# Node passes: new rows' transposes in banks of their own, aggregated rows' product at the pass's head, final rows copied ahead of the new normalisation

## The reference

```python
agg = segment_sum(alpha[:, :, None] * v[src], dst)          # first edge stage (attention)
embedding = agg.reshape(N, D) @ W0
h1 = _layer_norm(X + embedding, ln1_g, ln1_b)
ff = relu(h1 @ fc1_w + fc1_b) @ fc2_w + fc2_b                 # 128 -> 512 -> 128
x  = _layernorm(x + _layer_norm(h1 + ff, ln2_g, ln2_b))       # two normalisations in a row
# second edge stage: relu([x[src], edge_attr, req] @ W1 + b1) @ W2, summed by dst, both directions
# x[src] @ W1[:128] is formed once per node (y_tab) and gathered per edge
```

## Time and profile before

| | |
|---|---|
| Median of 3 runs | 2351.49 us (2351.31 to 2352.31) |
| The profiled execution's own time | 2351.63 us |
| Its span | 2349.8 us |
| First stage and attention edges | 0 to about 1137 us |
| Node passes | about 1137 to 1346.7 us |
| Second edge stage | 1346.7 us to the end |
| Mean granted TensorE clock | 0.77 of full speed |

### The profile page before, as it was taken

One profiled execution on the slowest core, in us unless ns is written; L12 is line 12 of the kernel. 1 busy time (PEld: TensorE's weight loads), 2 busy tenths in 40 slices (PEclk: granted clock), 3 DMA queues, 4 the chain that ended last, 5 costly groups with the idle time before them and its releaser, 6 DMA issues.

```text
span 2349.8 us, 31926 instructions
## 1 busy us (share of the span) xinstructions
PE 1416.0 (60%) x7352; PEld 1107.0 (47%) x7353; DVE 1439.1 (61%) x2963; ACT 742.3 (32%) x1515; POOL 1594.7 (68%) x1668
## 2 busy tenths in 40 slices
PE   5334655555555555555678566666666666666665
PEld 3134655555455555555566444444444444444443
DVE  2236977877877877878467444454554554554544
ACT  2143444344344344344366411111111111111111
POOL 4077777777777777776433277777777777777774
PEclk8667878777778778778799876877767777777776
DMA  5478555555555555555000122222222222222221
GB/s 166 127 180 275 174 157 165 162 156 164 163 156 166 161 156 164 162 156 154 11 33 33 47 60 63 65 63 63 65 64 62 65 64 63 64 64 65 62 64 46
DMA packets 149173, 255.39 MB, mean 109 GB/s; under 512 B 74829, under 2 KB 100097, under 8 KB 149005
## 3 DMA queue, kind: packets, MB, share of 16 engines
q0 software_dynamic: 65072, 160.39, 24.3%
q1 hardware_dynamic: 82194, 92.81, 12.8%
q10 hardware_dynamic: 1870, 1.78, 0.2%
HBM read 233.19 MB, written 28.04 MB: 111 GB/s over the span
## 4 chain that ended last, share of the span: by engine, by line
POOL 60%; issue 22%; PE 6%; DMA 5%; DVE 4%; ACT 2%; another core or an unknown queue 1%; POOLq 1%; DVEq 0%; ACTq 0%; PEldq 0%; SPq 0%
POOL arena L719 31%; POOL arena L662 29%; DMA kvq_tab<-arena 2%; PE ps L1120 2%; PE ps L1139 1%; DMA arena<-kvq_tab,arena 1%; PE ps L1079 1%; DMA arena<-in_src_dram 1%; ACT arena L875 1%; DVE arena L1508 1%; PE ps L1153 0%; DVE arena L1463 0%; PE ps L1115 0%; DVE arena L1525 0%
## 5 line engine op out<-in xcount | busy, mean ns | idle before, releaser
L662 POOL DMA_INDIRECT arena<-kvq_tab,arena x784 | 748.1, 954 | 266.4 <-issue 265.2
L719 POOL DMA_INDIRECT arena<-y_tab,arena x784 | 739.9, 944 | 251.9 <-issue 238.6
L1079 PE MATMUL ps<-arena 128*128 128x136 f32 x1568 | 314.0, 386 | 414.4 <-DVE arena L1463 414.4
L1079 PEld LDWEIGHTS ps<-arena 128*128 128x128 f32 x1568 | 304.3, 290 | 429.5 <-issue 429.5
L948 ACT ACTIVATE arena<-arena 128x512 f32<-128x512 f32 x224 | 123.3, 572 | 795.9 <-DVE arena L1596 795.9
L1596 DVE TENSOR_TENSOR arena<-ps,arena 128x512 f32<-128x512 f32 x224 | 134.7, 621 | 355.5 <-DMA arena<-y_tab,arena 352.5
L1225 PEld LDWEIGHTS ps<-arena 128*128 128x128 f32 x1568 | 268.3, 247 | 162.2 <-ACT arena L948 93.5
L1225 PE MATMUL ps<-arena 128*128 128x128 f32 x1568 | 289.7, 339 | 27.6 <-ACT arena L948 27.2
L1212 PE MATMUL ps<-w1blk,eaT 113*128 x456 | 255.8, 648 | 0.6 <-ACT eaT L943 0.6
L1409 DVE TENSOR_TENSOR arena<-ps,arena 128x512 f32<-128x512 f32 x224 | 137.8, 615 | 171.4 <-DMA arena<-kvq_tab,arena 163.8
L1055 PE MATMUL ps<-arena 128*128 128x128 f32 x1596 | 210.5, 285 | 44.5 <-ACT arena L811 27.7
(11 more groups left out here) (246 smaller groups left out, 1951.6 us busy)
## 6 DMA issues: line engine op xcount, KB each, us to landing
arena<-d SPq DMA_DIRECT2D x58, 897.0 KB
arena<-kvq_tab,arena POOLq DMA_INDIRECT x784, 2.8
arena<-y_tab,arena POOLq DMA_INDIRECT x784, 2.5
arena<-ea SPq DMA_DIRECT2D x60, 112.0 KB, 2.0
ea<-in_edge_attr_dram SPq DMA_DIRECT2D x2, 3125.0 KB, 19.1
y_tab<-arena SPq DMA_DIRECT2D x10, 625.0 KB
kvq_tab<-arena SPq DMA_DIRECT2D x6, 937.5 KB
arena<-kvq_tab SPq DMA_DIRECT2D x59, 64.0 KB
```

The lines of the kernel that those rows point to most:

```text
L662: g.indirect_dma_start(kv_s[:, r, t, :], None, kvq_tab.rearrange("n (a d) -> (n a) d", a=3), bass.IndirectOffsetOnAxis(ap=v3(idx, RING)[:, ...
L719: g.indirect_dma_start(yg_s[:, r, t, :], None, y_tab, bass.IndirectOffsetOnAxis(ap=v3(idx1, RING)[:, r, t:t + 1], axis=0)).then_inc(m_g[r] ...
L1079: last = mm(sums, hot_s[:, u, t, :], contrib_s[:, u, t * RW:(t + 1) * RW], start=(t == 0), stop=(t == G - 1))
```

## The change

- The transposes of `h1` go to banks 6 and 7, where the hidden blocks 1 and 3 also go, and wait for the relus of the pass before (`n_f1s`) where they waited for `n_xT`. ACT copies `nTh` from there.
- PE's product of the aggregated rows moves from between the hidden blocks to the head of the pass. It now waits for `n_xT` (banks 0 and 1 empty). For that ACT copies the rows of the next group (`nTa`) a pass earlier: after `res2` is normalised, ahead of the square root of the new group.
- ACT's copy of the transposed final rows (`nTx`) stands ahead of the normalisation into `h1`, where it stood behind it.
- `turn_rows` waits for the new semaphore `n_res` (DVE's add at line 1554 is done) and no longer for `n_v[0]` (its statistics are done), and for the copies of `y`.
- DVE's add at line 1554 waits for the copies of `y` as well.
- The loop runs six passes, and the seventh is written out, since its ACT part has no next group to copy. `s_bank` and `s_wu` are merged into `s_wq`.

```diff
-            with eng.Fori(0, GROUPS - 3) as i:
+            with eng.Fori(0, GROUPS - 4) as i:
                 one_pass(i + 3, i + 2, i + 1, i)
+            one_pass(GROUPS - 1, GROUPS - 2, GROUPS - 3, GROUPS - 4)
...
             def act_pass(new, mid, old, out_):
-                if new is not None:
+                if type(new) is int and new == 0:
                     a.activation(v3(nTa, GRP), by_tile(new), ACT.Copy).then_inc(n_aT, 1)
                 if mid is not None:
                     act.wait_ge(n_hTp, mid + 1)
-                    a.activation(nTh, bank(0, 2)[:, 0:GRP * P], ACT.Copy).then_inc(n_hT, 1)
+                    a.activation(nTh, bank(6, 2)[:, 0:GRP * P], ACT.Copy).then_inc(n_hT, 1)
...
+                if new is not None and not (type(new) is int and new == GROUPS - 1):
+                    act.wait_ge(n_emb, new + 1)
+                    a.activation(v3(nTa, GRP), by_tile(new + 1), ACT.Copy).then_inc(n_aT, 1)
                 if new is not None:
                     sqrt(0, new, norm1)
+                if old is not None:
+                    act.wait_ge(n_xTp, old + 2)
+                    act.wait_ge(n_x1c, old + 1)
+                    a.activation(nTx, bank(0, 2)[:, 0:GRP * P], ACT.Copy).then_inc(n_xT, 1)
+                if new is not None:
                     act.wait_ge(n_r[0], new + 1)
...
                     normalised(v3(h1, GRP), v3(res, GRP), norm1).then_inc(n_n1, 1)
-                if old is not None:
-                    act.wait_ge(n_xTp, old + 2)
-                    act.wait_ge(n_x1c, old + 1)
-                    a.activation(nTx, bank(0, 2)[:, 0:GRP * P], ACT.Copy).then_inc(n_xT, 1)
...
             def pe_pass(new, mid, old, out_):
+                if new is not None:
+                    if out_ is not None:
+                        pe.wait_ge(n_xT, out_ + 1)
+                        pe.wait_ge(n_ys, out_ + 1)
+                    if type(new) is int and 0 < new < 3:
+                        pe.wait_ge(n_res, new)
+                    pe.wait_ge(n_aT, new + 1)
+                    for t in range(GRP):
+                        last = mm(bank(0, 2)[0:NT, t * D:(t + 1) * D], nTa[:, t * NT:(t + 1) * NT], w0_sb[:, :])
+                    last.then_inc(n_emb, 1)
                 if mid is not None:
                     pe.wait_ge(n_n1, mid + 1)
-                    if out_ is not None:
-                        pe.wait_ge(n_xT, out_ + 1)
-                    transposes(h1, n_hTp)
+                    if not (type(mid) is int and mid == 0):
+                        pe.wait_ge(n_f1s, mid * FC)
+                    transposes(bank(6, 2), h1, n_hTp)
...
-                if out_ is not None:
-                    pe.wait_ge(n_ys, out_ + 2)
-                if new is not None:
-                    pe.wait_ge(n_aT, new + 1)
-                    for t in range(GRP):
-                        last = mm(bank(0, 2)[0:NT, t * D:(t + 1) * D], nTa[:, t * NT:(t + 1) * NT], w0_sb[:, :])
-                    last.then_inc(n_emb, 1)
...
-            def turn_rows(new, old):
-                if new is not None:
-                    pe.wait_ge(n_v[0], new + 1)
+            def turn_rows(new, old, out_):
+                if out_ is not None:
+                    pe.wait_ge(n_ys, out_ + 2)
+                if new is not None:
+                    pe.wait_ge(n_res, new + 1)
                 pe.wait_ge(n_x1, old + 1)
-                transposes(res2, n_xTp)
+                transposes(bank(0, 2), res2, n_xTp)
...
                     if mid is not None:
                         dve.wait_ge(n_n1, mid + 1)
-                    link(tt(r3, xg(new), v3(bank(0, 2)[:, 0:GRP * D], GRP), ALU.add))
+                    if out_ is not None:
+                        dve.wait_ge(n_ys, out_ + 2)
+                    tt(r3, xg(new), v3(bank(0, 2)[:, 0:GRP * D], GRP), ALU.add).then_inc(n_res, 1)
+                    dve.wait_ge(n_res, new + 1)
                     statistics(r3, n_v[0], norm1)
```

More of the change, by code:

```diff
@@ L251, in gnn_kernel @@
         s_tabi = [sem(f"s_tabi{l}") for l in range(2)]
-        s_dv = sem("s_dv"); s_wq = sem("s_wq"); s_init = sem("s_init"); s_bank = sem("s_bank"); s_wu = sem("s_wu")
+        s_dv = sem("s_dv"); s_wq = sem("s_wq"); s_init = sem("s_init");
         s_njc = sem("s_njc")
@@ L269, in gnn_kernel @@
         n_r = [sem(f"n_r{k}") for k in range(2)]
-        n_n1 = sem("n_n1"); n_xb = sem("n_xb")
+        n_n1 = sem("n_n1"); n_xb = sem("n_xb"); n_res = sem("n_res")
         n_b1 = sem("n_b1"); n_b1s = sem("n_b1s"); n_fc1 = sem("n_fc1"); n_hTp = sem("n_hTp")
@@ L986, in _ @@
             pe.wait_ge(s_const, 5)
-            pe.wait_ge(s_bank, 1)
-            pe.wait_ge(s_wq, 1)
+            pe.wait_ge(s_wq, 2)
             def pe_first(i):
@@ L1109, in _, with transposes @@
             pe.wait_ge(s_w4, 16 * (14 + 2 * (EG - 1)))
-            def transposes(src, done):
+            def transposes(to, src, done):
                 for t in range(GRP):
-                    last = tp(bank(0, 2)[:, t * P:(t + 1) * P], src[:, t * D:(t + 1) * D], ident[:, :])
+                    last = tp(to[:, t * P:(t + 1) * P], src[:, t * D:(t + 1) * D], ident[:, :])
                 last.then_inc(done, 1)
@@ L1136, in pe_pass @@
                     for t in range(GRP):
-                        if t == GRP - 1 and mid is not None:
-                            pe.wait_ge(n_hT, mid + 1)
                         last = mm(rows_y(t), nTx[:, t * P:(t + 1) * P], w1x[:, :])
@@ L1147, in pe_pass @@
                     hidden(mid, 1)
-                if out_ is not None:
-                    pe.wait_ge(n_ys, out_ + 2)
-                if new is not None:
-                    pe.wait_ge(n_aT, new + 1)
-                    for t in range(GRP):
-                        last = mm(bank(0, 2)[0:NT, t * D:(t + 1) * D], nTa[:, t * NT:(t + 1) * NT], w0_sb[:, :])
-                    last.then_inc(n_emb, 1)
-                if mid is not None:
                     for c in range(2, FC):
@@ L1158, in pe_pass @@
                         hidden(mid, c)
+                    if out_ is not None:
+                        pe.wait_ge(n_ys, out_ + 2)
                     for t in range(GRP):
                         if t == GRP - 2 and old is not None:
-                            turn_rows(new, old)
+                            turn_rows(new, old, out_)
                         for c in range(FC):
@@ L1269, in _ @@
             link = linker(dve, s_dv)
-            v.memset(ps[:, :], 0.0).then_inc(s_bank, 1)
+            v.memset(ps[:, :], 0.0).then_inc(s_wq, 1)
             dve.wait_ge(s_w, 48)
@@ L1362, in _ @@
             link(ts(epsc[:, :], epsc[:, :], 1.0, None, ALU.add))
-            ts(w2u[:, 2 * D:3 * D], w2wu[:, 2 * D:3 * D], epsc[:, :], None, ALU.mult).then_inc(s_wu, 1)
-            dve.wait_ge(s_wu, 1)
+            ts(w2u[:, 2 * D:3 * D], w2wu[:, 2 * D:3 * D], epsc[:, :], None, ALU.mult).then_inc(s_wq, 1)
+            dve.wait_ge(s_wq, 3)
             dve.wait_ge(s_init, 3)
```

## The result

The changed kernel takes 2342.61 us (median of 8 runs, 2340.02 to 2347.43); the kernel before took 2351.1 in its 8 runs beside it (2347.4 to 2352.31). The ratio worked out from the runs is 0.9974, with a 95% interval of 0.9964 to 0.9985: 6.1 us faster, between 3.5 and 8.5. (The two medians alone differ by 8.5 us, the far end of that interval.) On the 2351.49 of the forecast's basis that is 2345.4 us (2343.0 to 2348.0). The forecast was 2345.3.

A forecast was written before the change was run, and what follows sets the result against it. Bound: the chain from one group's `h1` to the next, with no engine full. Gains of 4.2 (six passes at 0.70), 1.7 (clock fall) and 0.4 (opening), 6.3 in all, take 2351.63 to 2345.3 us; range 2343.0 to 2349.0.

The forecast's parts named there:

- The steady pass: Loop passes of the node stage: period from 16.95 to 16.25, six times 0.70, 4.2 us in all.
- the extra copies: ACT's `nTa` (1.36) and `nTx` (0.68) ahead of `h1`: 0.6 of delay costs nothing, covered by POOL's L685.
- The 0.77 for the transposes: PE's transposes of `h1` in the steady pass before the change, given as 0.77 from start to start.
- The four hidden blocks: PE's hidden blocks in the changed steady pass, after `y`: 4.34, ending at 9.4 to 9.7.
- the wait added ahead of DVE's add: One more wait for DVE's add L1554 in each steady pass: worth up to 0.1, taken at 0.02.
- The fall of the clock: Half clock in the loop's second pass, 1.7 longer than its neighbours: taken to go, gaining 1.7.
- The earlier DVE: Rival: in steady passes L1518 starts before POOL's L690, period 0.26 shorter, six times 1.6, 2343.7; chance 0.10.
- The opening: Passes up to the third: transposes of `res2` start 0.3 earlier under `n_res`; gain 0.3 to 0.4, taken as 0.4.
- a rival, at 0.5: In the earlier-DVE rival (chance 0.10): half clock also ends sooner, so the opening may give 0.9, not 0.4: 2343.2.
- the seventh pass: Last of the six passes from the `h1` at 1199.44 to the last one, counted like the others at 0.70.
- The slower case: Rival: clock falls in every pass, period 18.95, six passes 10.3 longer, 2361.5; chance 0.05.
- the rival of a fall in another pass: The clock's fall stays or moves to another pass, price 1.7: 2346.2 to 2347.0; chance 0.20.

The follow-up runs named there:

- e3: Kernel before without POOL's addition of a bias to `h1c` (that part of the result missing); steady period 16.95, ratio to before 0.9989.
- e4: Changed kernel without POOL's addition of a bias to `h1c` (that part of the result missing); steady period 15.75, ratio to before 0.9947.
- e5: Kernel before with POOL's bias add to `xs` starting only after DVE's five-element instruction (one wait changed); period 15.94, ratio to before 0.9965.
- e6: Changed kernel with POOL's bias add to `xs` starting only after DVE's five-element instruction (one wait changed); period 15.78, ratio to before 0.9958.
- e10: The changed kernel run once more, nothing altered; steady period 16.27, ratio to before 0.9968.
- e1: Kernel before with only the transposes of `h1` in banks 6 and 7, product and ACT copies left in place; period 16.57, ratio to before 0.9989.
- e2: Changed kernel with ACT's copy of the final rows (`nTx`) behind the normalisation into `h1` again; period 17.46, ratio to before 1.0017.
- e7: Changed kernel with POOL's bias add a pass later and its copy into `nodes` after it, under DVE's statistics; period 15.25, ratio to before 0.9948.
- e8: e7 with the clearing of the second stage's two accumulators moved from POOL's first pass to its last; period 15.24, ratio to before 0.9913.
- e9: e8 with the copy of the next group's aggregated rows (`nTa`) on DVE instead of ACT; period 14.96, ratio to before 0.9924.
- e11: Changed kernel with PE's product of the aggregated rows put back between the hidden blocks; period 16.51, ratio to before 0.9998.

## Why the prediction was right, and where it was off

**The steady pass** came out as worked out, step by step. Transposes of `h1` at 2.16 (2.1 to 2.4 forecast), last relu at 9.77 (9.4 to 9.7, so it came 0.07 late), the data of the square root at 10.95 (10.98), the square root at 10.98 (11.03), the five instructions ending at 7.47 behind POOL's copy (7.49), the second square root 3.95 behind the first (3.95), L1525's counterpart ending with POOL's bias add (1231.17 and 1231.14), 5.28 from square root to `h1` (5.22), period 16.26 (16.25). That these agree for the reason given is shown by e3 and e4 (POOL's path binds after the change, not before) and by e5 and e6 (the bias add blocks 1.0 of 5.2, and it covers the 0.5 to 0.6 of the extra copies).

Three small terms in it were off and hardly show. The 0.77 for the transposes is a printed length and not, as the prediction says, from start to start, which is 0.61. The four hidden blocks take 4.65 from start to start and not 4.34, with the weights of a block waiting 0.25 for ACT's relu; both errors lie on the relu's side, which has slack. And the wait added ahead of DVE's add was taken at 0.02. Counted from the square root, the add starts at 0.92 where it started at 0.85, POOL's bias add at 3.59 where it was 3.51, and the next `h1` at 5.28 where it was 5.20: the wait costs 0.07 to 0.08, and all of it arrives. The square root came 0.05 before the forecast's 11.03, and so the period fits to 0.01.

**The fall of the clock** went, as forecast: the second of the loop's passes takes 16.32 at 1.00. Its gain, the fall and the steady gain together, is 2.31 of the forecast's 2.40.

**The earlier DVE** did not happen: its five instructions start at 4.11, and POOL's L691 at 3.96. It missed by 0.15.

**Two terms were mis-sized, both too small.** The opening was put at 0.4. The step said that PE is the bound until the last relu, "with the same work in another order"; but PE did that work at another clock. By the rows below half clock (0.50 granted) ended some 2 us sooner:

```profile
1181.08 3.13 PE L1171 MATMUL ps<-fc_sb,arena 128*128 128x128 f32 x16
1184.04 1.25 PE L1139 MATMUL ps<-w_sb,arena 128*125 128x128 f32 x10
1185.13 0.71 PE L1119 MATMUL ps<-ident,arena 128*128 128x128 f32 x5
```

That is the changed kernel. In the kernel before, the same product took 3.62, and the transposes of `h1` at 1184.15 still took 1.27:

```profile
1180.74 3.62 PE L1165 MATMUL ps<-fc_sb,arena 128*128 128x128 f32 x16
1184.15 1.27 PE L1115 MATMUL ps<-ident,arena 128*128 128x128 f32 x5
```

From the transposes of `res2` (1179.61 and 1179.98) to the second part of the last product PE needs 13.73 before and 12.53 after, 1.2 less for the same instructions; the transposes themselves stand 0.3 earlier against `h1`, and that is the forecast's 0.3. The sum, less 0.1 behind it, is the 1.4 of the table, and the changed kernel's other profile (e10) has 16.64 for this pass, 1.6 less than before. Why half clock ended sooner stays open. The prediction had this only inside a rival, at 0.5. The other term is the seventh pass, counted as a sixth like the others at 0.70. It gained 1.24 and takes 15.71, for it is now written out, and what its engines wait for are constants there, not values in registers. DVE's second add, L1553, starts 0.04 behind its predecessor and not 0.14, so the first square root comes 0.10 earlier. L1564 follows its scales at once (1291.65 after 1291.54) where in the loop it idles 0.20, so the statistics end 0.26 earlier after the square root; POOL's bias add follows them after 0.08 and not 0.19, and `h1` follows L1533 after 0.04 and not 0.12. The second square root comes 3.17 behind the first instead of 3.95, since no copy of a next group stands ahead of it. But that is not what shortens the pass: POOL's bias add still holds L1533 to the end, as in the loop.

```profile
1294.21 1.56 POOL L686 TENSOR_TENSOR xs<-xs,rows 128x640 f32<-128x640 f32 x1 [7.29 <-DVE arena L1519]
...
1294.71 1.07 DVE L1533 SCALAR_TENSOR_TENSOR arena<-arena 128x5 f32<-128x5 f32 x1
```

The four parts make 0.55 of the 0.56 by which the pass is shorter than its neighbours. They are read from this one trace; no run changes the waits alone. The opening and the seventh pass gave 1.5 more than forecast.

**What came in on the other side** was costed at nothing. The stage starts at half clock in the changed kernel's profile: the same eight products, ahead of any changed instruction, take 1.87

```profile
1136.94 1.87 PE L1186 MATMUL ps<-ln_cols,fc_sb 128*128 128x1 f32 x8 [0.81 <-ACT mark L860]
```

where they took 1.23 before:

```profile
1136.99 1.23 PE L1178 MATMUL ps<-ln_cols,fc_sb 128*128 128x1 f32 x8 [0.81 <-ACT mark L859]
```

That is the +0.6 up to the first `h1`. The three experiments built from the kernel before (e1, e3, e5) have 1.13 to 1.15 there; of the eight built from the changed kernel, four (e2, e7, e8, e10) have 1.86 or 1.87 and four (e4, e6, e9, e11) 1.05 to 1.26. So it is no fixed cost of the change, and whether the change makes it likelier stays open. The +0.5 behind the last `res2` is the last product of the oldest group (L1151), which takes 4.63 where it took 4.20, at a clock that had fallen in either kernel. Entry and exit together (+1.1) and the two gains (-1.5) nearly cancel, and so the total of 6.65 in the profiled execution is near the 6.3 forecast. That closeness is partly luck: the terms of the steady pass and of the fall were right, those of the opening, the seventh pass and the two ends were wrong by 0.5 to 1 us each. The ratio of the runs gives 6.1, as near; the two medians differ by 8.5.

**The rivals.** The slower case needed the clock to fall in every pass; after the change it fell in none. Where it was seen to fall in a loop pass (the second in before and e3, the third and seventh in e2, the fifth in e11, one profile each), PE had a pause of 1.95 to 2.57 in every pass; in the changed kernel, e1 and e4 to e10 the longest steady pause is 1.4 and no loop pass behind the first is under 1.00. That goes with the step taken, but a single profile of each doesn't prove it. What the prediction takes from the Trainium skill beside the rival of a fall in another pass stands in the section "What's actually happening" of TensorE: Matmul & The Clock Gate: one kernel shows different numbers of slow products, by the phase at its start. The passes in which the fall came here differ too, but so do the kernels.

## What to carry to other kernels

Behind a wait that a change removes, look for the next chain at its own time (here 0.77 ahead of the first, which was all that could be gained), and ask first which engine's finish it ends with: a one-word change in when POOL starts gave as much as the reordering of three engines. Costs that are covered are only lent: count them when the cover goes. And a pass that leaves the loop is another pass (here 0.56 shorter); cost it, and the clock at the edges of the stage, apart from the steady ones.

## What the hardware showed

**A five-element DVE instruction waits for the end of a POOL instruction.** L1525 takes 0.17 alone and 1.17 under POOL's 128x640 addition, so the size of DVE's instruction says nothing of what the overlap costs. Not every POOL instruction does this. In the opening of the changed kernel:

```profile
1152.98 10.73 POOL L693 MEMSET arena<- 128x12756 f32 x1
...
1161.22 0.17 DVE L1533 SCALAR_TENSOR_TENSOR arena<-arena 128x5 f32<-128x5 f32 x1
...
1163.65 5.40 POOL L694 MEMSET arena<- 2x6378 f32 x1
...
1166.74 5.69 DVE L1526 TENSOR_SCALAR arena<-arena 128x128 f32<-128x128 f32 x5
```

Under a memset the five-element instruction takes its 0.17, while the five normalising ones, which take 1.38 alone, are not done when the memset ends 2.31 after their start, and, with two additions of POOL behind it, take 5.69. The Trainium skill (SBUF — State Buffer, section "Who interferes with whom") says that a VectorE instruction with two SBUF inputs contends with a GpSimd instruction that reads SBUF and not with one that only writes it, while the 2-port modes of `tensor_scalar` contend in either case; the rows agree on both. DVE's statistics, and its additions with an input in PSUM, run beside POOL at their usual length (e8: L1521 1.07 and L1569 0.82 under POOL's L687), and that is where e7 to e9 put POOL's work.

**Waits on register values in a hardware loop cost DVE up to 0.2 ahead of one instruction.** L1564, with three such waits, has "[0.20 <-issue]" in each loop pass and no idle time where the pass is written out and the waits are for constants. Its counterpart before, L1554, has two and starts 0.13 behind its predecessor in the loop, and at once in the third pass, which is written out.

**The same kernel took 2351 us in two groups of runs and 2732 in two others.** The changed kernel, run in both sorts, has the first two stages' end at 1137 us in one and near 1320 in the other, and its second edge stage takes 1002.9 and 1202.2 us. POOL is as busy in both (739.9 and 740.4 us in that stage), and the node passes, which gather nothing, take the same time to 0.2 us. What grows is POOL's waiting ahead of its gathers:

```profile
POOL arena L663 <- remote: 179.3, 53, 5.3
POOL arena L720 <- remote: 131.4, 34, 7.5
```

These two rows, of its waits in the slower group (us in total, times, longest), have no counterpart in the faster one. The second and the third group ran on a chip of the same number, the one at 2351 and the other at 2734, so that number doesn't settle it. Whether the chip, its memory or something beside it was the cause, no run here tells.
